# Attention scores and masks as 128x32 column tiles, score tiles apart within a turn, narrow diagonal blocks sharing a PSUM bank

## Chip, cores and metric

One Trainium2 chip, one of its NeuronCores. The metric is the device time of one execution in microseconds: the median of three runs of the kernel before is 1314.45 us (1314.13 to 1315.17).

## What is computed

`x` is (1, 2048, 128) in fp32. Six sublayers follow each other, each on a layer-normalised `x` and added to it; the two expert layers and the two ternary layers are weighted by 0.5:

```python
x = x + 0.5 * expert_ffn(layernorm(x), ...)      # 8 experts, top 1, gelu, then layernorm
x = x + attention0(layernorm(x), wq, wk, wv, wo, bo)
x = x + 0.5 * expert_ffn(layernorm(x), ...)
x = x + 0.5 * ternary_ffn(layernorm(x), ...)
x = x + attention1(layernorm(x), W, b)           # no output projection
x = x + 0.5 * ternary_ffn(layernorm(x), ...)
```

Both attentions have 16 heads of dimension 8 over 2048 positions and are causal:

```python
scores = einsum('bhqd,bhkd->bhqk', q, k)
scores = where(tril(ones((t, t), bool)), scores, -inf)
attn = softmax(scores / sqrt(8), axis=-1)
ctx = einsum('bhqk,bhkd->bhqd', attn, v)
```

## The kernel before, in words

The change lies in the two calls of `attention_layer`. Its heads are worked in four groups of four (`G`), its queries in four chunks of 512 (`CH`, `NCH`); a pair of group and chunk (g, c) is a *step*. `STEPS` has 16 of them: chunks 0 to 3 for groups 0 and 1, then chunks 3 to 0 for groups 2 and 3.

Queries and keys lie in `q_slots` and `k_slots` as fp16 parts, 32 partitions (`SLOT`) for each head of a group. In `k_slots` the rows of the three other heads are zero, so that a matmul over all 128 rows gives one head's scores.

A step needs two things.

*Maxima.* For each query of the step the largest score must be known before the exponentials. TensorE computes scores a first time with queries on the partitions, in *units* of one 128-query block, one head and up to 512 keys (`max_units_of`, line 1202; on the diagonal a mask matmul behind it, line 1205), and VectorE reduces each unit with a maximum (line 1317). A unit on the diagonal is 128, 256, 384 or 512 wide, with its block i. The maxima are turned by TensorE (line 1210), split into fp16 parts by VectorE and sent by DMA into spare rows of `q_slots`, from where the second score matmul subtracts them. Units go round a ring of three PSUM banks, 5 to 7 (`ring_item`): TensorE waits before a unit until the one three places earlier is read.

*Quads.* A quad is 128 keys for the 512 queries of the step, for its four heads; a step has 4(c+1) of them, the last four on the diagonal and 512, 384, 256 and 128 columns wide. `score_tile(q, pr)` computes scores of two heads with keys on the partitions, as two row tiles of 32 rows (line 1162), into two banks; diagonal ones get a mask matmul over all rows each (line 1169). ScalarE takes the exponential of both banks in one instruction (line 1279). `values(q)` multiplies with the values, four heads as column tiles of 9 columns, fp32, into one bank (line 1182). Score tiles alternate between two pairs of banks; a tile waits for the exponential of the tile two before (`exp_done`).

At the end of a step its output is copied by ScalarE (line 1287), turned by TensorE (line 1225), and scaled by VectorE (lines 1344 and 1348).

TensorE's order is written out in `TURNS`: one quad a turn, with some units of later steps. `units_beside_quads` deals them out: a unit costs `UNIT_FIXED` plus its columns, a quad `QUAD_FIXED` plus its columns, and the units of a step have to be done three quads (`SLACK`) before it begins. Units of the first two steps go ahead of all quads. In a turn stand the two score tiles, three quarters of the ring's items, the values of the quad before, and the last quarter. VectorE and ScalarE follow the same lists. Projections of queries, keys and values run ahead of the turns and beside the first of them.

Of the kernel before, what the change touches and what calls it, by code (L numbers as in the profile page):

```python
# [9 lines left out]
ALU = mybir.AluOpType  # L10
ACT = mybir.ActivationFunctionType
AX = mybir.AxisListType

P = 128
# [3 lines left out]
CH = 512  # L18
NCH = T // CH
BPC = CH // P  # L20
H = 16
DH = D // H
G = 4
# [10 lines left out]
TERMS = 3  # L34
Q_PARTS, K_PARTS = (0, 1, 0), (0, 0, 1)
SLOT = 32
MAX_ROW = TERMS * DH
MAX_PARTS = 2
MAX_UNIT = 16384.0
# [23 lines left out]
def macaron_layers(nc, x_in, wq, wk, wv, wo, bo, wr, w1, b1, wo2, bo2, gamma, beta,  # L63
# [16 lines left out]
    with stack:  # L80
        blk = stack.enter_context(nc.Block())
        psum = stack.enter_context(nc.psum_tensor("psum", [P, 8, CH], F32))
# [924 lines left out]
                [(g, c) for c in reversed(range(NCH)) for g in range(HALF, NG)]  # L1007
        AHEAD = 2
        SLACK = 3
        UNIT_FIXED, QUAD_FIXED = 64, 64  # L1010

        def quads_of(step):
            return [(step, j) for j in range(BPC * (step[1] + 1))]

        def max_units_of(step):

            return [(step, i, kc, h) for i in range(BPC) for kc in range(step[1] + 1) for h in range(G)]

        def columns_of_quad(q):
            (_, c), j = q  # L1020
            return CH - max(0, j - BPC * c) * P

        def columns_of_unit(u):
            (_, c), i, kc, _ = u
            return CH if kc < c else (i + 1) * P

        def units_beside_quads():

# [31 lines left out]
        def attention_layer(proj, layer, projected, given, next_norms, next_given, released):  # L1060
# [17 lines left out]
            def rows_of(h):  # L1078
                return slice(SLOT * h, SLOT * (h + 1))

# [58 lines left out]
            for (_, units), (_, turn_max, _, turn_out) in zip(TURNS, PLAN):  # L1139
# [3 lines left out]
                for item in RING_ITEMS[-1]:  # L1143
                    ring_no[item] = len(ring_no)
            last_unit = {s: max(n for item, n in ring_no.items() if item[0] == "scores" and item[1][0] == s)
                         for s in STEPS}

            @blk.tensor
            def _(pe):
                def score_tile(q, pr):  # L1150

                    (g, c), j = q
                    n = quad_no[q]
                    off = first_query(q)
                    if j == 0 and pr == 0:
                        pe.wait_ge(negmax_landed[step_no[q[0]] % 4], 16 * MAX_PARTS * (step_no[q[0]] // 4 + 1))
                    tile = 2 * n + pr
                    if tile >= 2:
                        pe.wait_ge(exp_done, tile - 1)
                    for par in range(2):  # L1160
                        rows = rows_of(2 * pr + par)
                        last = pe.matmul(psum[:, S_BANKS + 2 * (tile % 2) + par, off:CH],  # L1162
                                         k_slots[rows, G * g + 2 * pr + par, j * P:(j + 1) * P],
                                         q_slots[rows, g, c * CH + off:(c + 1) * CH],
                                         start=True, stop=q not in diagonal)
                    if q in diagonal:

                        for par in range(2):
                            last = pe.matmul(psum[:, S_BANKS + 2 * (tile % 2) + par, off:off + P],  # L1169
                                             ident_bf[:, :], later_keys[:, :], start=False, stop=True)  # L1170
                    last.then_inc(scores_done, 1)

                def values(q):

                    (g, c), j = q
                    n = quad_no[q]
                    off = first_query(q)
                    pe.wait_ge(exp_done, 2 * n + 2)
                    if j == 0:
                        pe.wait_ge(*((out_copied, step_no[q[0]]) if step_no[q[0]] else (o_bank_set, 1)))  # L1180
                    for h in range(G):
                        last = pe.matmul(psum[VW * h:VW * h + DH + 1, O_BANK, off:CH],  # L1182
                                         v_aug[:, j, G * g + h, :],
                                         probs[:, (2 * n + h // 2) % NP, h % 2, off:CH],
                                         start=(j == 0), stop=(j == BPC * (c + 1) - 1))
                    last.then_inc(pv_done, 1)

                def ring_item(item):
                    kind, what = item
                    n = ring_no[item]  # L1190
                    bank = RING_BANKS + n % RING
                    if n >= RING:
                        pe.wait_ge(ring_read, n - RING + 1)
                    if kind == "scores":
                        (g, c), i, kc, h = what
                        if (g, i, kc, h) == (0, 0, 0, 0):
                            pe.wait_ge(q_landed[c], 16 if c else 16 * (G + 1))
                            if c:
                                pe.wait_ge(k_landed[c - 1], 16 * G)
                        w = CH if kc < c else (i + 1) * P  # L1200
                        qb = BPC * c + i
                        last = pe.matmul(psum[:, bank, 0:w], q_slots[:, g, qb * P:(qb + 1) * P],  # L1202
                                         k_slots[:, G * g + h, kc * CH:kc * CH + w], start=True, stop=kc < c)
                        if kc == c:
                            last = pe.matmul(psum[:, bank, i * P:w], later_keys[:, :], ident_bf[:, :],  # L1205
                                             start=False, stop=True)
                    elif kind == "max":
                        k = step_no[what]
                        pe.wait_ge(negmax_ready, k + 1)
                        last = pe.transpose(psum[0:G * BPC, bank, 0:P], neg_max[:, k % 2, :], ident[:, :])  # L1210
                    elif kind == "turned":
                        pe.wait_ge(ring_read, ring_no["out", (NG - 1, what)] + 1)
# [24 lines left out]
                for turn, ((q, _), items) in enumerate(zip(TURNS, RING_ITEMS)):  # L1237
                    if turn == LAST_PROJECTION:
                        proj.transposes(pe, NCH - 1)
                        proj.queries_keys(pe, NCH - 1)  # L1240
                        proj.values(pe, NCH - 1)
                    if turn == LAST_PROJECTION + 1:

                        pe.wait_ge(proj.lo_ready, 2 * NCH)
                        pe.wait_ge(proj.v_ready, NCH)

                    cuts = [0, 0, len(items) // 2 + len(items) // 4, len(items)]
                    if q:
                        score_tile(q, 0)
                    for item in items[cuts[0]:cuts[1]]:  # L1250
                        ring_item(item)
                    if q:
                        score_tile(q, 1)
                    for item in items[cuts[1]:cuts[2]]:
                        ring_item(item)
                    if previous:
                        values(previous)
                    for item in items[cuts[2]:cuts[3]]:
                        ring_item(item)
                    previous = q  # L1260

# [28 lines left out]
            def _(dve):  # L1290
# [8 lines left out]
                for turn, (items, (m_now, _, _, _)) in enumerate(zip(RING_ITEMS, PLAN)):  # L1299
# [8 lines left out]
                    for item in items:  # L1308
# [2 lines left out]
                        bank = RING_BANKS + n % RING  # L1311
                        dve.wait_ge(ring_full, n + 1)
                        if kind == "scores":
                            s, i, kc, h = what
                            dst = part_max[:, step_no[s] % 2, h, i, kc:kc + 1]
                            w = CH if kc < s[1] else (i + 1) * P
                            dve.tensor_reduce(dst, psum[:, bank, 0:w], axis=AX.X, op=ALU.max).then_inc(ring_read, 1)  # L1317
                        elif kind == "turned":
                            dve.tensor_copy(ctx_t[:, what * CH:(what + 1) * CH], psum[:, bank, :]).then_inc(ring_read, 1)
                        elif kind == "project":  # L1320
# [128 lines left out]
```

## Time and profile before

| | us |
|---|---|
| median of three runs | 1314.45 |
| profiled execution | 1314.37 |
| its span | 1312.6 |
| TensorE busy in it | 1186.3 |
| VectorE busy | 1033.5 |
| ScalarE busy | 668.8 |

The profile is of one execution. Busy is the time covered by an engine's instructions; matmuls are pipelined and their ends modelled, so that the distance between two starts says more than the length of one. TensorE's granted clock was 0.97 of the full one in the mean. The first attention layer covers about 191 to 652 us of the span, the second 835 to 1290 us.

### The profile page before, as it was taken

The numbers are of one execution on the slowest core, as the hardware profiler recorded it, in microseconds if no ns is written. First come the engines' busy times: TensorE is split into PE (matmuls) and PEld (weight loads), VectorE is DVE, ScalarE is ACT, GpSimd is POOL, SyncE is SP. The second block draws the span as 40 slices with busy tenths as digits, with TensorE's granted clock in tenths as the row PEclk, the third lists the DMA queues.
The fourth block names the chain that finished last, engine by engine and source line by source line (L and its number), as shares of the span: only waits on it lengthen the run. The fifth ranks groups of instructions, "written<-read, shape, count | busy, mean of one in ns | idle before, by whom it ended". The sixth has DMA issues, their size and how long they took to land.

```text
span 1312.6 us, 21461 instructions
## 1 busy us (share of the span) xinstructions
PE 1186.3 (90%) x8293; PEld 461.7 (35%) x8293; DVE 1033.5 (79%) x2503; ACT 668.8 (51%) x861; POOL 65.3 (5%) x62
## 2 busy tenths in 40 slices
PE   1899968999999999999699979599999999999997
PEld 1455533222222222333355547232222222222336
DVE  8976487899999897875547566789999999877664
ACT  1322114555677667766332224145556667777663
POOL 5111010000000000000101000100000000000000
PEclk9999988999999999999799979799999999999999
DMA  4100141000000000000000000420000000000001
GB/s 147 33 1 1 48 121 57 1 2 1 2 1 1 2 1 1 1 1 2 1 0 1 1 0 25 146 57 1 1 2 1 1 1 1 1 1 2 1 2 33
DMA packets 23506, 23.26 MB, mean 18 GB/s; under 512 B 3134, under 2 KB 21220, under 8 KB 23404
## 3 DMA queue, kind: packets, MB, share of 16 engines
q1 hardware_dynamic: 22252, 18.73, 4.9%
q0 software_dynamic: 1152, 3.15, 0.9%
q8 instruction: 66, 1.08, 0.3%
q14 instruction: 36, 0.29, 0.1%
HBM read 13.20 MB, written 8.39 MB: 16 GB/s over the span
## 4 chain that ended last, share of the span: by engine, by line
PE 69%; DVE 25%; issue 2%; ACT 2%; DMA 1%; SPq 0%; DVEq 0%; ACTq 0%
PE psum L1182 19%; PE psum L1202 17%; DVE part_max L1317 14%; PE psum L442 9%; PE psum L1162 8%; PE psum L1169 4%; PE psum L466 2%; PE psum L898 2%; PE psum L1205 2%; PE psum L913 1%; DVE xn L167 1%; DVE norm_v L150 1%; PE psum L427 1%; DVE parts L838 1%; PE psum L1225 1%
## 5 line engine op out<-in xcount | busy, mean ns | idle before, releaser
L1317 DVE TENSOR_REDUCE part_max<-psum 128x1 f32<-128x512 f32 (+3 forms) x1280 | 703.5, 604 | 118.2 <-PE psum L1205 59.4
L1279 ACT ACTIVATE hidden<-psum 128x1024 f32<-128x1024 f32 (+3 forms) x640 | 542.4, 895 | 311.1 <-PE psum L1169 166.1
L1202 PE MATMUL psum<-k_slots,q_slots 128*128 128x512 f16 (+3 forms) x1280 | 396.8, 359 | 43.5 <-DVE part_max L1317 24.4
L1182 PE MATMUL psum<-hidden,v_aug 128*9 128x512 f32 (+3 forms) x2560 | 296.1, 535 | 0.0
L1202 PEld LDWEIGHTS psum<-k_slots,q_slots 128*128 128x128 f16 x1280 | 111.5, 97 | 402.0 <-DVE part_max L1317 320.0
L442 PE MATMUL psum<-parts,w_parts 128*128 128x512 f16 x768 | 177.6, 382 | 1.9 <-DVE parts L838 1.9
L1162 PE MATMUL psum<-q_slots,k_slots 32*128 32x512 f16 (+3 forms) x1280 | 163.9, 355 | 7.2 <-ACT hidden L1279 4.6
L1205 PE MATMUL psum<-ident_bf,later_keys 128*128 128x128 bf16 x512 | 111.0, 227 | 0.0
L442 PEld LDWEIGHTS psum<-parts,w_parts 128*128 128x128 f16 x768 | 73.2, 99 | 80.9 <-issue 3.0
L586 ACT CAST parts<-psum 128x512 f16<-128x512 f32 x64 | 37.2, 588 | 106.7 <-PE psum L427 106.7
L1162 PEld LDWEIGHTS psum<-q_slots,k_slots 32*128 32x128 f16 x1280 | 46.3, 91 | 109.4 <-issue 52.1
L1169 PE MATMUL psum<-later_keys,ident_bf 128*128 128x128 bf16 x512 | 73.8, 226 | 0.0
L1182 PEld LDWEIGHTS psum<-hidden,v_aug 128*9 128x9 f32 x2560 | 38.1, 88 | 72.3 <-issue 49.3
L838 DVE TENSOR_TENSOR parts<-parts 128x1024 f16<-128x1024 f16 x64 | 45.7, 738 | 18.3 <-ACT parts L586 18.2
L1205 PEld LDWEIGHTS psum<-ident_bf,later_keys 128*128 128x128 bf16 x512 | 51.9, 101 | 3.3 <-issue 0.3
L1169 PEld LDWEIGHTS psum<-later_keys,ident_bf 128*128 128x128 bf16 x512 | 29.2, 97 | 38.8 <-issue 27.1
L624 POOL TENSOR_TENSOR x_plus<-xn,bo_bc 128x512 f32<-128x512 f32 x8 | 13.8, 1720 | 566.1 <-DVE xn L167 527.4
L466 PE MATMUL psum<-wo_sb,hidden 128*128 128x128 f32 x256 | 33.3, 294 | 3.7 <-ACT hidden L577 3.7
L466 PEld LDWEIGHTS psum<-wo_sb,hidden 128*128 128x128 f32 x256 | 32.9, 209 | 5.6 <-ACT hidden L577 4.7
L953 POOL TENSOR_TENSOR x_plus<-x_res,fb_half 128x512 f32<-128x512 f32 x8 | 10.0, 1265 | 495.6 <-DVE xn L167 495.6
L244 ACT COPY xn_t<-psum 128x512 f32<-128x512 f32 x8 | 4.7, 587 | 58.2 <-PE psum L219 58.2
L675 DVE TENSOR_TENSOR x_plus<-psum,x_plus 128x512 f32<-128x512 f32 x8 | 5.5, 690 | 35.4 <-PE psum L466 35.4
(168 smaller groups left out, 735.7 us busy)
## 6 DMA issues: line engine op xcount, KB each, us to landing
q_slots<-q_rows SPq DMA_DIRECT2D x8, 512.0 KB, 3.8
k_slots<-k_rows POOLq DMA_DIRECT2D x24, 128.0 KB, 4.1
q_rows<-parts SPq DMA_DIRECT2D x18, 128.0 KB, 2.7
k_rows<-parts SPq DMA_DIRECT2D x18, 128.0 KB, 2.4
q_slots<-in_L_ffn_W_dram SPq DMA_DIRECT2D x2, 1024.0 KB, 6.6
k_slots<-k_rows SPq DMA_DIRECT2D x8, 128.0 KB, 4.0
q_slots<-nm_parts SPq DMA_DIRECT2D x64, 4.0 KB
out_dram<-x_res SPq DMA_DIRECT2D x4, 256.0 KB, 2.3
```

Source lines behind the costliest of these rows:

```text
L442: last = pe.matmul(psum[:, t, :], w1_parts[:, e, wp, t * P:(t + 1) * P], x_mask[:, k % NX, xp, :], start=(e == 0 and (wp, xp) == (0, 0)), ...
L466: last = pe.matmul(psum[:, DOWN_BANK, i * D:(i + 1) * D], hidden[:, n % 2, t, i * P:(i + 1) * P], wo2_sb[:, t, :], start=(t == 0), stop=(t ...
L586: act.copy(mask_sb[:, k % NX, :], psum[:, MASK_BANKS + k % 2, :]).then_inc(mask_ready, 1)
L838: dve.tensor_tensor(x_mask[:, k % NX, :, :], x_parts[:, n % 2, :, :], mask_sb[:, k % NX, :].rearrange("p (a t) -> p a t", a=1).broadcast_t ...
L898: last = pe.matmul(psum[:, 6 + n % 2, i * D:(i + 1) * D], hidden[:, n % 2, t, i * P:(i + 1) * P], tw2_t[:, t, :], start=(t == 0), stop=(t ...
L1162: last = pe.matmul(psum[:, S_BANKS + 2 * (tile % 2) + par, off:CH], k_slots[rows, G * g + 2 * pr + par, j * P:(j + 1) * P], q_slots[rows, ...
L1169: last = pe.matmul(psum[:, S_BANKS + 2 * (tile % 2) + par, off:off + P], ident_bf[:, :], later_keys[:, :], start=False, stop=True)
L1182: last = pe.matmul(psum[VW * h:VW * h + DH + 1, O_BANK, off:CH], v_aug[:, j, G * g + h, :], probs[:, (2 * n + h // 2) % NP, h % 2, off:CH] ...
L1202: last = pe.matmul(psum[:, bank, 0:w], q_slots[:, g, qb * P:(qb + 1) * P], k_slots[:, G * g + h, kc * CH:kc * CH + w], start=True, stop=kc ...
L1205: last = pe.matmul(psum[:, bank, i * P:w], later_keys[:, :], ident_bf[:, :], start=False, stop=True)
L1279: act.activation(probs[:, tile % NP, :, off:CH], psum[:, bank:bank + 2, off:CH], ACT.Exp, scale=scale).then_inc(exp_done, 1)
L1317: dve.tensor_reduce(dst, psum[:, bank, 0:w], axis=AX.X, op=ALU.max).then_inc(ring_read, 1)
```

## The change

- Every score matmul of attention, in units and in quads, and every mask matmul on it is split into four, one for each 32 columns of its stationary operand (`COLS` = 4), which go to the four quarters of the partitions. Quads use all 128 rows instead of 32.
- A score tile has the mask of its first head ahead of the scores of its second.
- On the diagonal, four heads of a 128-wide unit or two of a 256-wide one share a bank, with one mask matmul (of four tiles) and one reduce.
- In a turn: first score tile, a third of the ring's items, second score tile, a third, the values of the quad before, the last third.
- `UNIT_FIXED`, `QUAD_FIXED` go from 64, 64 to 100, 500, and a unit's columns include its mask and heads.

```diff
-        UNIT_FIXED, QUAD_FIXED = 64, 64
+        UNIT_FIXED, QUAD_FIXED = 100, 500
...
+        def unit_width(step, i, kc):
+
+            return CH if kc < step[1] else (i + 1) * P
+
         def max_units_of(step):
 
-            return [(step, i, kc, h) for i in range(BPC) for kc in range(step[1] + 1) for h in range(G)]
+            units = []
+            for i in range(BPC):
+                for kc in range(step[1] + 1):
+                    heads = CH // unit_width(step, i, kc)
+                    units += [(step, i, kc, h, heads) for h in range(0, G, heads)]
+            return units
...
         def columns_of_unit(u):
-            (_, c), i, kc, _ = u
-            return CH if kc < c else (i + 1) * P
+            step, i, kc, _, heads = u
+            return heads * (unit_width(step, i, kc) + (P if kc == step[1] else 0))
...
+            def rows32(m):
+                return slice(SLOT * m, SLOT * (m + 1))
+
+            def diagonal_part(rows, heads):
+
+                return rows.rearrange("p (a k) -> p a k", a=heads)[:, :, -P:]
+
+            def repeated(mask, heads):
+
+                return mask[:, :].rearrange("p (a k) -> p a k", a=1).broadcast_to([P, heads, P])
...
                     for par in range(2):
-                        rows = rows_of(2 * pr + par)
-                        last = pe.matmul(psum[:, S_BANKS + 2 * (tile % 2) + par, off:CH],
-                                         k_slots[rows, G * g + 2 * pr + par, j * P:(j + 1) * P],
-                                         q_slots[rows, g, c * CH + off:(c + 1) * CH],
-                                         start=True, stop=q not in diagonal)
-                    if q in diagonal:
-
-                        for par in range(2):
-                            last = pe.matmul(psum[:, S_BANKS + 2 * (tile % 2) + par, off:off + P],
-                                             ident_bf[:, :], later_keys[:, :], start=False, stop=True)
+                        bank = S_BANKS + 2 * (tile % 2) + par
+                        for m in range(COLS):
+                            last = pe.matmul(psum[rows32(m), bank, off:CH],
+                                             k_slots[:, G * g + 2 * pr + par, j * P + m * SLOT:j * P + (m + 1) * SLOT],
+                                             q_slots[:, g, c * CH + off:(c + 1) * CH],
+                                             start=True, stop=q not in diagonal)
+                        if q in diagonal:
+                            for m in range(COLS):
+                                last = pe.matmul(psum[rows32(m), bank, off:off + P],
+                                                 ident_bf[:, rows32(m)], later_keys[:, :], start=False, stop=True)
...
-                        last = pe.matmul(psum[:, bank, 0:w], q_slots[:, g, qb * P:(qb + 1) * P],
-                                         k_slots[:, G * g + h, kc * CH:kc * CH + w], start=True, stop=kc < c)
+                        for a in range(heads):
+                            for m in range(COLS):
+                                last = pe.matmul(psum[rows32(m), bank, a * w:(a + 1) * w],
+                                                 q_slots[:, g, qb * P + m * SLOT:qb * P + (m + 1) * SLOT],
+                                                 k_slots[:, G * g + h0 + a, kc * CH:kc * CH + w],
+                                                 start=(a == 0), stop=(kc < c))
                         if kc == c:
-                            last = pe.matmul(psum[:, bank, i * P:w], later_keys[:, :], ident_bf[:, :],
-                                             start=False, stop=True)
+                            for m in range(COLS):
+                                last = pe.matmul(diagonal_part(psum[rows32(m), bank, 0:heads * w], heads),
+                                                 later_keys[:, rows32(m)], repeated(ident_bf, heads),
+                                                 start=False, stop=True)
...
-                    cuts = [0, 0, len(items) // 2 + len(items) // 4, len(items)]
+                    cuts = [len(items) // 3, 2 * len(items) // 3]
...
-                            dst = part_max[:, step_no[s] % 2, h, i, kc:kc + 1]
-                            w = CH if kc < s[1] else (i + 1) * P
-                            dve.tensor_reduce(dst, psum[:, bank, 0:w], axis=AX.X, op=ALU.max).then_inc(ring_read, 1)
+                            w = unit_width(s, i, kc)
+                            dve.tensor_reduce(part_max[:, step_no[s] % 2, h0:h0 + heads, i, kc],
+                                              psum[:, bank, 0:heads * w].rearrange("p (a k) -> p a k", a=heads),
+                                              axis=AX.X, op=ALU.max).then_inc(ring_read, 1)
```

## Rows read from the trace of the kernel before

**Rows 1.** The page: busy time of each engine, share of span, instructions.
```profile
PE 1186.3 (90%) x8293; PEld 461.7 (35%) x8293; DVE 1033.5 (79%) x2503; ACT 668.8 (51%) x861; POOL 65.3 (5%) x62
```

**Rows 2.** The page: chain that ended last, by engine and by line.
```profile
PE 69%; DVE 25%; issue 2%; ACT 2%; DMA 1%; SPq 0%; DVEq 0%; ACTq 0%
PE psum L1182 19%; PE psum L1202 17%; DVE part_max L1317 14%; PE psum L442 9%; PE psum L1162 8%; PE psum L1169 4%; PE psum L466 2%; PE psum L898 2%; PE psum L1205 2%; PE psum L913 1%; DVE xn L167 1%; DVE norm_v L150 1%; PE psum L427 1%; DVE parts L838 1%; PE psum L1225 1%
```

**Rows 3.** Stretches of the second attention layer: length, busy us (instructions), clock, DMA share, GB/s.
```profile
835.00:862.00 27.00, 18.68 (x115) 7.76 (x115) 22.73 (x64) 7.78 (x10) 4.35 (x8) 0.87 0.39 107
862.00:889.10 27.10, 25.14 (x203) 8.61 (x195) 24.61 (x51) 12.93 (x18) 0.00 (x0) 1.00 0.02 4
889.10:940.30 51.20, 47.18 (x343) 14.47 (x340) 45.99 (x91) 28.00 (x36) 0.00 (x0) 1.00 0.01 1
940.30:1011.00 70.70, 67.84 (x486) 19.11 (x485) 65.69 (x123) 43.79 (x53) 0.00 (x0) 1.00 0.00 1
1011.00:1175.70 164.70, 161.86 (x1175) 43.87 (x1173) 146.93 (x268) 116.57 (x134) 0.00 (x0) 1.00 0.01 1
1175.70:1234.00 58.30, 57.22 (x449) 17.50 (x445) 45.02 (x90) 42.36 (x51) 0.00 (x0) 1.00 0.01 1
1234.00:1273.30 39.30, 37.27 (x333) 12.53 (x333) 22.88 (x72) 26.77 (x38) 0.59 (x1) 0.99 0.01 2
1273.30:1289.70 16.40, 11.89 (x74) 4.99 (x71) 12.04 (x60) 7.25 (x13) 3.21 (x3) 0.81 0.01 1
```

**Rows 4.** Groups by shape: count, busy us, mean ns of one, idle before, releasers.
```profile
L1317 DVE TENSOR_REDUCE part_max<-psum 128x1 f32<-128x512 f32 x896 | 566.9, 684 | 75.4 <-PE psum L1202 52.4 <-PE psum L1205 18.8
...
L1169 PE MATMUL psum<-later_keys,ident_bf 128*128 128x128 bf16 x512 | 73.8, 226 | 0.0
...
L1317 DVE TENSOR_REDUCE part_max<-psum 128x1 f32<-128x128 f32 x128 | 31.7, 285 | 15.6 <-PE psum L1205 15.1
```

**Rows 5.** Timeline of a c=3 turn: start us, us, engine, line, count, idle before.
```profile
1150.08 1.94 ACT L1279 ACTIVATE hidden<-psum 128x1024 f32<-128x1024 f32 x2 [0.75 <-PE psum L1162]
...
1150.30 0.12 PEld L1182 LDWEIGHTS psum<-hidden,v_aug 128*9 128x9 f32 x8 [0.23 <-issue]
...
1151.70 2.48 DVE L1317 TENSOR_REDUCE part_max<-psum 128x1 f32<-128x512 f32 x4 [0.36 <-PE psum L1202]
...
1151.82 0.65 PE L1162 MATMUL psum<-q_slots,k_slots 32*128 32x512 f16 x4
...
1152.24 1.02 ACT L1279 ACTIVATE hidden<-psum 128x1024 f32<-128x1024 f32 x1 [0.22 <-PE psum L1162]
```

**Rows 6.** Timeline of TensorE's matmuls alone through a full turn.
```profile
1044.98 1.04 PE L1182 MATMUL psum<-hidden,v_aug 128*9 128x512 f32 x8
1045.96 0.39 PE L1202 MATMUL psum<-k_slots,q_slots 128*128 128x512 f16 x1
1046.18 0.60 PE L1225 MATMUL psum<-ident,xn_t 128*128 128x128 f32 x4
1046.71 0.39 PE L1162 MATMUL psum<-q_slots,k_slots 32*128 32x512 f16 x4
1047.04 0.97 PE L1202 MATMUL psum<-k_slots,q_slots 128*128 128x512 f16 x3
1047.94 0.62 PE L1182 MATMUL psum<-hidden,v_aug 128*9 128x512 f32 x4
```

**Rows 7.** Chain of waits, in order of time: start us, us, what.
```profile
756.46 10.36 PE psum L442 x48
```

**Rows 8.** Timeline of TensorE's matmuls in a diagonal turn.
```profile
1261.53 0.39 PE L1162 MATMUL psum<-q_slots,k_slots 32*128 32x512 f16 x2
1261.85 0.29 PE L1169 MATMUL psum<-later_keys,ident_bf 128*128 128x128 bf16 x2
...
1262.60 0.41 PE L1182 MATMUL psum<-hidden,v_aug 128*9 128x128 f32 x8
```

**Rows 9.** Who waited for whom, 835 to 1290 us: total us, times, longest.
```profile
PEld psum L1202 <- DVE part_max L1317: 158.9, 303, 0.9
```

**Rows 10.** Stretch of the first attention layer, last two steps, columns as rows 3.
```profile
630.70:651.90 21.20, 15.95 (x106) 7.76 (x104) 9.98 (x34) 7.34 (x12) 3.69 (x3) 0.67 0.00 1
```

More of the change, by code:

```diff
@@ L36 @@
 SLOT = 32
+COLS = P // SLOT
 MAX_ROW = TERMS * DH
@@ L1194, in ring_item @@
                     if kind == "scores":
-                        (g, c), i, kc, h = what
-                        if (g, i, kc, h) == (0, 0, 0, 0):
+                        (g, c), i, kc, h0, heads = what
+                        if (g, i, kc, h0) == (0, 0, 0, 0):
                             pe.wait_ge(q_landed[c], 16 if c else 16 * (G + 1))
@@ L1199, in ring_item @@
                                 pe.wait_ge(k_landed[c - 1], 16 * G)
-                        w = CH if kc < c else (i + 1) * P
+                        w = unit_width(*what[:3])
                         qb = BPC * c + i
-                        last = pe.matmul(psum[:, bank, 0:w], q_slots[:, g, qb * P:(qb + 1) * P],
-                                         k_slots[:, G * g + h, kc * CH:kc * CH + w], start=True, stop=kc < c)
+                        for a in range(heads):
[4 more added lines that the diff above has]
+                                                 start=(a == 0), stop=(kc < c))
                         if kc == c:
-                            last = pe.matmul(psum[:, bank, i * P:w], later_keys[:, :], ident_bf[:, :],
-                                             start=False, stop=True)
+                            for m in range(COLS):
+                                last = pe.matmul(diagonal_part(psum[rows32(m), bank, 0:heads * w], heads),
+                                                 later_keys[:, rows32(m)], repeated(ident_bf, heads),
+                                                 start=False, stop=True)
                     elif kind == "max":
@@ L1245, in _ @@
                         pe.wait_ge(proj.v_ready, NCH)
-                    cuts = [0, 0, len(items) // 2 + len(items) // 4, len(items)]
+                    cuts = [len(items) // 3, 2 * len(items) // 3]
                     if q:
                         score_tile(q, 0)
-                    for item in items[cuts[0]:cuts[1]]:
+                    for item in items[:cuts[0]]:
                         ring_item(item)
@@ L1253, in _ @@
                         score_tile(q, 1)
-                    for item in items[cuts[1]:cuts[2]]:
+                    for item in items[cuts[0]:cuts[1]]:
                         ring_item(item)
@@ L1257, in _ @@
                         values(previous)
-                    for item in items[cuts[2]:cuts[3]]:
+                    for item in items[cuts[1]:]:
                         ring_item(item)
@@ L1313, in _ @@
                         if kind == "scores":
-                            s, i, kc, h = what
-                            dst = part_max[:, step_no[s] % 2, h, i, kc:kc + 1]
-                            w = CH if kc < s[1] else (i + 1) * P
-                            dve.tensor_reduce(dst, psum[:, bank, 0:w], axis=AX.X, op=ALU.max).then_inc(ring_read, 1)
+                            s, i, kc, h0, heads = what
+                            w = unit_width(s, i, kc)
+                            dve.tensor_reduce(part_max[:, step_no[s] % 2, h0:h0 + heads, i, kc],
+                                              psum[:, bank, 0:heads * w].rearrange("p (a k) -> p a k", a=heads),
+                                              axis=AX.X, op=ALU.max).then_inc(ring_read, 1)
                         elif kind == "turned":
```

## The prediction

> **What bounds the kernel now.** I read the busy shares first: TensorE is busy 90% of the span, VectorE 79%, ScalarE 51% [rows 1]. The chain of waits puts 69% on TensorE and 25% on VectorE; the ring's unit matmuls (L1202), the value matmuls (L1182), the score matmuls (L1162) and VectorE's reduce (L1317) lead it, all of them in attention [rows 2]. Then I cut the second attention layer into its stages [rows 3]: the run-in (835 to 862), the steps with c=0, c=1, c=2 of the first two groups, the four steps with c=3, and c=2, c=1, c=0 of the last two groups. From 862 to 1011 us VectorE is busy 90 to 93% of each stage and TensorE 92 to 96%; in the c=3 steps TensorE has 98%, VectorE 89%; behind them TensorE has 95 to 98% and VectorE 58 to 77%. So VectorE sets the pace early, TensorE late. Of VectorE's time the reduces are most: 684 ns for 512 columns, 285 for 128 [rows 4]; four in a row take 2.48 us, so one follows the other after (2.48-0.68)/3 = 0.60 us, some 0.08 before the other's end. I count 608 and 208 ns, and on the line between them 475 and 341 for 384 and 256 columns [rows 4, 5]. ScalarE needs 2 x 0.92 us of a full turn (two exponentials 1.94 us, one 1.02) [rows 5]; it bounds nothing but a short tail.
>
> The timeline of TensorE shows what a turn holds [rows 6]. 48 expert matmuls of 512 columns take 10.36 us, 0.213 us each: 2.4 columns a ns, the upper clock [rows 7]. Value matmuls are column tiles already: two groups of four take 1.04 us, one (cut by the window's end) 0.62, so a group follows another after some 0.43 us. 512 fp32 columns stream 0.427 (two passes: transposes of 128 fp32 columns follow each other after 0.109): four tiles cost what one does, and a few ns, 7 by the 1.04 us of the eight. The four score matmuls are row tiles, and also run together: from their start to the next unit 0.33 us, of which 0.213 is stream. The rest is the price of changing the tiling: about 0.10 us each time. Transposes to scores (0.53 - 0.44), scores to unit (0.33 - 0.21), and values to unit (0.98 - 0.87) agree [rows 6].
>
> **The change, part by part.** The counts are worked out from the code's planner and its two cost formulas; per layer there are 16 steps, 160 turns, of them 64 diagonal.
>
> (1) Tiling changes. A turn with units has four (rows, full, columns, full), a diagonal one two more, because a mask lies between score tiles [rows 8]. That makes 752 a layer before, 74 us at 98 ns, some 147 us in both. After, only transposes and projections are of another tiling: I keep 0.65 us a step for them (0.44 stream, two changes).
>
> (2) Score matmuls. Four heads at once become four heads one after the other, each as a group of four column tiles over all 128 rows. A full turn streams 4 x 0.213 instead of 0.213: +0.64 us, less four changes (0.39): +0.25. Diagonal turns paired only two heads and so go from 2w to 4w columns: for w = 512 from 1.07 us ([rows 8], 1261.53 to 1262.60) to (2048+512)/2.4 = 1.07, so the wide one gains just the two changes around the values, and narrower ones more. Over a layer score streams go from 51 to 130 us (masks in both).
>
> (3) Unit matmuls. Columns stay: four tiles together stream what one 128-wide matmul did. Units per layer go from 640 to 560, since four 128-wide or two 256-wide heads share a bank. A reduce over four blocks costs 608 ns instead of 4 x 208, over two blocks 608 instead of 2 x 341: 0.30 us less a step, 5 us a layer, of VectorE. If the blocks cost the reduce something, the bound is the four short ones, so between 0 and 5.
>
> (4) Group overhead. A layer will have about 2030 groups of four. Between value groups 7 ns are over the stream, between full matmuls 2 [rows 6, 7]; I take 5, so 10 us a layer. Bounds: 2 ns (4 us), and 28 ns, if each of four tiles added its 7 (57 us). The values' eight loads come within 0.12 us, of which 0.09 is one [rows 5]: 4 ns for 9 columns, so 32 columns may need 16 and a group 64, where 128-column groups (some 510 a layer) stream 53; at worst 6 us of the 10.
> The Trainium skill (TensorEngine Tiling (Array Packing), Restrictions) says that column tiling turns fast weight load off, and TensorE: Matmul & The Clock Gate (LDWEIGHTS) gives P/1.2 ns for P columns. By that 32 columns take 27 ns; what it would do is rival C.
>
> (5) The order. Score tiles stand a third of the turn's units apart, and the values behind two thirds. Today the second tile sometimes waits for the exponential of the turn before: four score matmuls then cover 0.65 us instead of 0.39 [rows 5, 6]. After, the tiles are over 0.6 us apart and ScalarE needs 0.92, within a turn of 2.4: this goes. The planner's new costs (100 and 500) give a diagonal quad more weight, so units come evenly: 3 to 5 a turn in the c=3 steps, where now one turn has 7 and another 2. TensorE's loads for units stand 159 us of the layer behind the reduce [rows 9]; most is cover by matmuls in flight, but bursts of units against a 0.6 us reduce are what makes TensorE stop.
>
> **The sum**, second layer. TensorE's load is stream (columns by 2400 a us), changes and 0.65 a step, after with 5 ns a group. The c=3 steps show it: before 51.5 units + 17.9 scores + 49.5 values + 288 changes, 28.2, + 2.6 = 149.8 (rounded); after 52.1 + 52.9 + 49.5 + 2.6 + 747 groups, 3.7 = 160.8. In a c=2 stage scores and changes go from 7.3 + 11.0 to 19.6, in late c=1 from 5.5 + 7.8 to 12.8; values (17.9 and 11.1) stay, units move by under 1. Run-in and first c=0, 54.1 us: reduces 35.1 before, 35.5 after; no change. First c=1, 51.2: reduces 42.9 to 43.9, TensorE 42 to 43: no change, the even order against 1 us more. First c=2, 70.7: reduces 61.5 to 59.1, TensorE 60.3 to 62.7, so both near 63: -1.5. The c=3 steps, 164.7: TensorE 149.8 to 160.8, VectorE busy 146.9 as before. This stage is now 15 us above its heavier load, 0.23 us a turn, in waits of the kind of (5); I let it be 5 above after (0.08 a turn, a choice: the waits of single score tiles and bursts go): 166, +1.3. Late c=2, 58.3: TensorE 53.1 to 55.4, 5.2 above becomes 1.8: -1.1. Late c=1, 39.3: 34.5 to 34.1, 4.8 above becomes 2.2: -3. Last c=0, 16.4: 11.2 to 10.6 and no split waits: -1. That is -5.3 a layer; the first layer has a longer tail (21 us for 16 [rows 10]), so -6.5 there. Sum -12. Nothing outside attention changes. The profiled execution took 1314.37 us around its span of 1312.6 and lies within 0.1 us of the median, so 1314.4 - 12 = **1302**.
>
> **Rivals.**
> A, the forecast: 1302, own range 1288 to 1312.
> B, more is won: groups cost 2 ns and TensorE runs nearly without waits. 6 us a layer from the groups, 5 from the c=3 steps: 1302 - 24 = 1278. For: late stages at 98% busy. Against: early VectorE sets the time.
> C, weights late (slower). Where a 128-column group streams 53 ns and the next group's four loads take longer, TensorE waits. At twice the 53, 510 groups x 54 ns = 27 us a layer, of which some 60% where TensorE decides: 1302 + 33 = 1335. For: the second of two masks starts 0.29 - 0.226 = 0.064 us behind the first, where it streams 0.053: a load that was not ready shows [rows 4, 8]. Against: the 4 ns of nine columns [rows 5]. It makes the change a loss from 10 ns over the stream a group, about. This is also where the skill's 27 ns a load lead; no run here shows it yet.
> D, waits stay (slower). TensorE's added 11 us in the c=3 steps come on top of unchanged waits: +11 there, +2.3 late c=2, +1 first c=2, 0 elsewhere: +13 a layer, 1340. It decides from 0.16 us of waits a turn. For: each TensorE stop on the ring also delays scores that stand behind it. Against: the waits come with bursts.
> E, instruction rate. A layer will hold 8,130 matmuls and as many loads, 16,260 instructions for 6,140: one in 26 ns over its 427 us, against 70 now; a narrow diagonal turn about 110 in 1.5 us. Nothing in the trace shows sequences that dense for long; eight loads in 0.12 us show it only for a short one. At 32 ns each a layer takes 520 us and the kernel about 1500; if only diagonal turns are held (28 ns x 110 = 3.1 us, +0.7 for each of 128) 1302 + 90 = 1392, which I take. That fp16 column tiles did not run together at all would cost far more (every score and unit stream fourfold); the fp32 ones speak against it.
> The skill (TensorE: Matmul & The Clock Gate, Part 2) names some 62 ns a MATMUL where the sequencer's microcode decodes; 8,130 of them would be 504 us a layer. Nothing here tells whether that path is on.
> F, nothing moves: loads trade evenly, 1314.
>
> **Chances.** A 0.47 (0.42 faster, 0.05 same), B 0.15, C 0.10, D 0.15 (0.02 of it same), E 0.08, F 0.05. Under 0.2%, 2.6 us, a measurement can't tell the kernels apart: faster 0.57, same 0.12, slower 0.31. The range 1274 to 1342 leaves E and a strong B out.
>
> **What would show it.** TensorE from a unit to scores or values with no 0.1 us over the stream; groups 218 ns apart at 512 columns and 58 at 128 (C: over 80); a full turn with three units near 2.4 us; single score tiles never waiting for ScalarE; reduces of 512 columns at 600 ns with four outputs; late c=1 near 36 us, c=3 near 166. The prediction is wrong if c=3 steps lengthen by over 5 us a layer (D, or C if narrow groups are late), or if gaps appear between groups that wait for nothing (E).

## The result and the profile after

The changed kernel takes 1263.18 us (median of 4 runs, 1262.68 to 1264.19) against 1314.29: a ratio of 0.9619, 95% interval [0.9595, 0.9644], 51 us less. 1302 was forecast, and 1274 was the low end of the range: the direction was right, the size four times too small.

The page of the profile after (span 1260.9 us): busy time by engine; chain that ended last.

```profile
PE 1160.4 (92%) x18405; PEld 589.2 (47%) x18405; DVE 1017.0 (81%) x2343; ACT 670.0 (53%) x861; POOL 65.4 (5%) x62
...
PE 70%; DVE 24%; issue 2%; ACT 2%; DMA 1%; SPq 0%; DVEq 0%; ACTq 0%
```

TensorE holds 18,405 matmuls instead of 8,293 and is busy for less time [rows 1]; the two engines share the chain as before [rows 2].

The stages of the second attention layer (columns as in rows 3). Here and in rows 3 every cut lies 11.1 us behind the first exponential of the stage's first step, in the kernel before and in the changed one alike. So the lengths are those from one first exponential to the next, but the busy times belong to a stretch that lies 11.1 us late:

```profile
832.90:857.00 24.10, 23.16 (x493) 10.90 (x485) 23.59 (x46) 13.56 (x18) 0.00 (x0) 1.00 0.03 7
857.00:904.50 47.50, 46.30 (x938) 21.29 (x938) 46.07 (x84) 28.23 (x35) 0.00 (x0) 1.00 0.01 3
904.50:969.70 65.20, 64.75 (x1238) 28.90 (x1230) 61.59 (x109) 42.75 (x52) 0.00 (x0) 1.00 0.01 3
969.70:1131.50 161.80, 161.52 (x3016) 73.01 (x3012) 147.42 (x251) 117.02 (x134) 0.00 (x0) 1.00 0.01 3
1131.50:1187.40 55.90, 55.74 (x1155) 26.77 (x1151) 43.38 (x76) 41.53 (x50) 0.00 (x0) 1.00 0.01 3
1187.40:1222.10 34.70, 33.59 (x814) 17.47 (x806) 20.97 (x59) 27.32 (x39) 0.66 (x1) 1.00 0.02 4
1222.10:1236.00 13.90, 9.47 (x113) 4.61 (x112) 11.49 (x56) 6.38 (x11) 3.14 (x3) 0.72 0.00 1
```

Against [rows 3] each stage is shorter:

| stage | forecast | measured |
|---|---|---|
| first c=0 | 0 | 27.1 to 24.1: -3.0 |
| first c=1 | 0 | 51.2 to 47.5: -3.7 |
| first c=2 | -1.5 | 70.7 to 65.2: -5.5 |
| c=3, four steps | +1.3 | 164.7 to 161.8: -2.9 |
| late c=2 | -1.1 | 58.3 to 55.9: -2.4 |
| late c=1 | -3 | 39.3 to 34.7: -4.6 |
| last c=0 | -1 | 16.4 to 13.9: -2.5 |

That is -24.6 for this layer where I had -5.3; the first layer went from 437 to 412 us, and some 2 us more lie outside the two.

Cut at the exponentials themselves, the first three stages together ("early" below) and the c=3 steps are, before:

```profile
850.87:999.84 148.97, 138.58 (x1004) 42.02 (x1003) 134.59 (x259) 80.75 (x101) 2.17 (x4) 1.00 0.05 14
999.84:1164.53 164.69, 161.93 (x1175) 44.19 (x1175) 148.30 (x273) 115.86 (x133) 0.00 (x0) 1.00 0.01 1
```

and after:

```profile
821.78:958.54 136.76, 133.60 (x2737) 61.47 (x2732) 131.78 (x237) 81.84 (x101) 2.17 (x4) 1.00 0.06 17
958.54:1120.31 161.77, 161.48 (x3015) 73.17 (x3010) 147.93 (x252) 115.74 (x132) 0.00 (x0) 1.00 0.01 3
```

Early, VectorE's busy time fell from 134.6 to 131.8 us, and its idle time from 14.4 to 5.0.

TensorE's matmuls in a full turn of the c=3 steps of the changed kernel (start us, us, engine, line, count):

```profile
1021.75 1.03 PE L1203 MATMUL psum<-hidden,v_aug 128*9 128x512 f32 x8
1022.61 0.60 PE L1225 MATMUL psum<-k_slots,q_slots 128*32 128x512 f16 x8
1023.04 0.60 PE L1184 MATMUL psum<-q_slots,k_slots 128*32 128x512 f16 x8
1023.47 0.39 PE L1225 MATMUL psum<-k_slots,q_slots 128*32 128x512 f16 x4
1023.69 0.60 PE L1184 MATMUL psum<-q_slots,k_slots 128*32 128x512 f16 x8
```

From the values to the unit are 0.86 us, which is the stream of two fp32 groups (2 x 0.427) and nearly nothing else; two fp16 groups take 0.43, one 0.21 to 0.22. No change of tiling is left ([rows 6]: 0.98, 0.33). And the narrowest diagonal turn of a late c=1 step, where 128-column groups follow each other:

```profile
1208.93 0.23 PE L1231 MATMUL psum<-ident_bf,later_keys 128*32 128x128 bf16 x4
1208.99 0.23 PE L1184 MATMUL psum<-q_slots,k_slots 128*32 128x128 f16 x4
1209.04 0.23 PE L1190 MATMUL psum<-later_keys,ident_bf 128*32 128x128 bf16 x4
...
1209.38 0.23 PE L1190 MATMUL psum<-later_keys,ident_bf 128*32 128x128 bf16 x4
1209.43 0.60 PE L1203 MATMUL psum<-hidden,v_aug 128*9 128x256 f32 x8
```

Nine groups, 36 matmuls and 36 loads, take 0.50 us: 55 ns a group of 53 ns of stream, 7 ns an instruction. With this, rival C (loads late, over 80 ns a group) and rival E (26 ns an instruction too dense) are out. The reduce takes the shared banks at the price of a full one (count, busy us, mean ns, idle before):

```profile
L1343 DVE TENSOR_REDUCE part_max<-psum 128x1 f32<-128x512 f32 x896 | 564.9, 683 | 52.5 <-PE psum L1225 28.5 <-PE psum L1231 16.6
...
L1343 DVE TENSOR_REDUCE part_max<-psum 128x2 f32<-128x512 f32 x64 | 42.6, 686 | 9.3 <-PE psum L1231 8.7
...
L1343 DVE TENSOR_REDUCE part_max<-psum 128x4 f32<-128x512 f32 x32 | 22.1, 689 | 9.5 <-PE psum L1231 9.3
```

Two or four outputs instead of one cost 3 and 6 ns.

### The profile page after: what moved, and what is told of

It is laid out like the page before. It is cut to its first block, busy times and chain, and to the rows that moved or that the text cites. A ratio compares the mean times of both kernels' runs of the same rounds, so it can differ in the third digit from the quotient of the medians.

```text
span 1260.9 us, 41528 instructions
## 1 busy us (share of the span) xinstructions
PE 1160.4 (92%) x18405; PEld 589.2 (47%) x18405; DVE 1017.0 (81%) x2343; ACT 670.0 (53%) x861; POOL 65.4 (5%) x62
## 4 chain that ended last, share of the span: by engine, by line
PE 70%; DVE 24%; issue 2%; ACT 2%; DMA 1%; SPq 0%; DVEq 0%; ACTq 0%
PE psum L1203 16%; PE psum L1184 15%; DVE part_max L1343 14%; PE psum L1225 13%; PE psum L443 11%; PE psum L467 3%; PE psum L899 2%; PE psum L1231 2%; PE psum L1190 1%; PE psum L914 1%; PE psum L1252 1%; DVE xn L168 1%; PE psum L428 1%; DVE norm_v L151 1%; ACT hidden L1306 1%
## 5 line engine op out<-in xcount | busy, mean ns | idle before, releaser
L1343 DVE TENSOR_REDUCE part_max<-psum 128x1 f32<-128x512 f32 (+3 forms) x1120 | 688.9, 668 | 86.0 <-PE psum L1231 48.0
L1225 PE MATMUL psum<-k_slots,q_slots 128*32 128x512 f16 (+3 forms) x5120 | 410.4, 353 | 20.5 <-DVE nm_parts L1364 7.1
L1184 PE MATMUL psum<-q_slots,k_slots 128*32 128x512 f16 (+3 forms) x5120 | 355.8, 349 | 4.5 <-ACT hidden L1306 1.4
L1225 PEld LDWEIGHTS psum<-k_slots,q_slots 128*32 128x32 f16 x5120 | 130.8, 97 | 244.7 <-DVE part_max L1343 126.5
L1184 PEld LDWEIGHTS psum<-q_slots,k_slots 128*32 128x32 f16 x5120 | 127.8, 97 | 105.1 <-ACT hidden L1306 15.9
L1190 PE MATMUL psum<-later_keys,ident_bf 128*32 128x128 bf16 x2048 | 103.2, 220 | 0.0
L1231 PE MATMUL psum<-ident_bf,later_keys 128*32 128x128 bf16 (+2 forms) x1408 | 92.1, 252 | 0.0
L1203 PEld LDWEIGHTS psum<-hidden,v_aug 128*9 128x9 f32 x2560 | 61.3, 91 | 41.1 <-issue 1.5
L1190 PEld LDWEIGHTS psum<-later_keys,ident_bf 128*32 128x32 bf16 x2048 | 55.1, 97 | 13.8
L1231 PEld LDWEIGHTS psum<-ident_bf,later_keys 128*32 128x32 bf16 x1408 | 38.6, 100 | 28.9 <-issue 18.1
```

The source lines that it names most:

```text
L1184: last = pe.matmul(psum[rows32(m), bank, off:CH], k_slots[:, G * g + 2 * pr + par, j * P + m * SLOT:j * P + (m + 1) * SLOT], q_slots[:, g, ...
L1190: last = pe.matmul(psum[rows32(m), bank, off:off + P], ident_bf[:, rows32(m)], later_keys[:, :], start=False, stop=True)
L1225: last = pe.matmul(psum[rows32(m), bank, a * w:(a + 1) * w], q_slots[:, g, qb * P + m * SLOT:qb * P + (m + 1) * SLOT], k_slots[:, G * g + ...
L1231: last = pe.matmul(diagonal_part(psum[rows32(m), bank, 0:heads * w], heads), later_keys[:, rows32(m)], repeated(ident_bf, heads), start=Fa ...
L1343: dve.tensor_reduce(part_max[:, step_no[s] % 2, h0:h0 + heads, i, kc], psum[:, bank, 0:heads * w].rearrange("p (a k) -> p a k", a=heads), ...
```

## The experiments

All ratios are to the kernel before, run on the same chip; the brackets are 95% intervals, so that a difference of two ratios is uncertain by 4 to 5 us. "Early" is the stretch from the second layer's first exponential to the first of its c=3 steps: 149.0 us in the kernel before, of them 14.4 in which VectorE idles, and 136.8 and 5.0 in the changed one.

### The changed kernel less one part

**The turn's order put back.**

```diff
-                    cuts = [len(items) // 3, 2 * len(items) // 3]
+                    cuts = [0, 0, len(items) // 2 + len(items) // 4, len(items)]
```

(and the old loop over them)

> The changed kernel (1263) with only the turn's order put back: both score tiles first, three quarters of the items, values, the last quarter. Theory 1 (the new order evens what reaches VectorE, and that took its idle time out of the early stages): VectorE's idle in the stages c=0, c=1, c=2 of the first groups, 5 us a layer in the changed kernel against 13 before, comes back, and single score tiles wait for ScalarE again: 1263 + 2 x 8 + 4 = about 1283. Rival 2 (the lost tiling changes alone shortened the blocks between units, so the order is worth nothing): within 4 us of 1263.

Measured 1274.9 us, ratio 0.9726 [0.9701, 0.9752]: some 14 us lost, between the two. Early 139.4 us, VectorE idle 7.7; the c=3 steps 163.0. The order is worth something, but seven tenths of the early idle time that went stay away without it. The weight loads of the score tiles wait 24 us for ScalarE instead of 16 over the whole run.

**The planner's old costs.**

```diff
-        UNIT_FIXED, QUAD_FIXED = 100, 500
+        UNIT_FIXED, QUAD_FIXED = 64, 64
...
-            return heads * (unit_width(step, i, kc) + (P if kc == step[1] else 0))
+            return heads * unit_width(step, i, kc)
```

> The changed kernel with the planner's old costs (64 and 64, a unit's mask not counted). Theory 1 (even numbers of units a turn matter): turns with 6 to 8 units beside turns with 2 return and with them waits on the ring, some 3 us a layer early and 2 late: about 1273. Rival 2 (the ring and VectorE's pace smooth it anyway): within 4 us of 1263.

1260.3 us, 0.9609 [0.9587, 0.9631]: no loss. Theory 1 is wrong here; the even numbers of units that I counted on buy nothing.

**One head to a bank.**

```diff
-                    heads = CH // unit_width(step, i, kc)
+                    heads = 1
```

> The changed kernel with one head to a bank for every unit, as before. VectorE gets back 5 us of reduces a layer, of which about half falls where VectorE sets the time: theory 1 expects 1263 + 2 x 3 = 1269. Rival 2 (shared banks also hold more work in the ring of three, and that took VectorE's idle out of the early stages): 1263 + 2 x (3 + 6) = about 1281.

1274.0 us, 0.9717 [0.9693, 0.9741]: 13 us lost, between the two. Early 140.8 us, but idle 5.0: in the new tiling the banks' part shows as VectorE's busy time (135.8 against 131.8), not as idle.

**Full matmuls, no column tiles.**

```diff
-                        for m in range(COLS):
-                            last = pe.matmul(psum[rows32(m), bank, off:CH],
-                                             k_slots[:, G * g + 2 * pr + par, j * P + m * SLOT:j * P + (m + 1) * SLOT],
+                        last = pe.matmul(psum[:, bank, off:CH],
+                                         k_slots[:, G * g + 2 * pr + par, j * P:(j + 1) * P],
```

(and so for masks and units)

> The changed kernel with units and scores as full 128x128 matmuls over 128 rows; the values stay column tiles. Same stream, a quarter of the matmuls, two changes of tiling a turn (into and out of the values). If a change of tiling costs 0.1 us and nothing else differs: TensorE's load +160 x 0.196 = 31 us a layer, of which the late 22 us count in full and the early third: 1263 + 2 x 25 = 1313, that is about the time of before. Rival (four column tiles give more than the absence of changes, or less): below 1295 if the changes hide under waits.

1307.7 us, 0.9952 [0.9933, 0.997]: 44 us lost, 50 expected. Early and the c=3 steps:

```profile
847.32:989.29 141.97, 139.31 (x984) 53.97 (x983) 133.22 (x237) 81.75 (x101) 2.17 (x4) 1.00 0.05 14
989.29:1162.28 172.99, 172.99 (x1152) 60.82 (x1151) 148.78 (x252) 115.75 (x132) 0.00 (x0) 1.00 0.01 1
```

Early, VectorE idles 8.8 us. TensorE is busy without a gap in the c=3 steps, +11.2 us for 64 turns with two changes, 0.175 us a turn. Column tiles are not faster than one full matmul (the same stream); they pay because the values are column tiles in any case and everything else can then be too.

**Only the units full.** As above, for units and their masks alone.

> The changed kernel with only the units as full matmuls, the scores left as column tiles: up to six changes of tiling a turn. TensorE's load +160 x 0.59 = 94 us a layer, less in the last turns without units: 1263 + 2 x 75 = about 1410. If the changes cost TensorE only where it would not wait anyway: 1340 to 1380.

1418.4 us, 1.0797 [1.0776, 1.0819], two executions: near the 1410 expected for up to six changes a turn.

### The kernel before with one part

**The order alone** (the first edit of this section the other way round, on the old tiling).

> The kernel before with only the new order of a turn, its tiling kept. Row tiles of the four heads no longer run together: each full turn streams scores twice (+0.213 us) and changes tiling twice more (+0.20). TensorE's load rises by 96 x 0.41 + 64 x 0.2 (diagonal turns: two changes back and forth with units between tiles), 40 to 52 us a layer, partly under VectorE early: 1314 + 2 x 35 = about 1385. Rival: the even order wins back what VectorE waits early (13 us a layer): 1314 + 2 x 22 = 1358.

1345.8 us, 1.0245 [1.0224, 1.0265], two executions: slower, and less so than either said. The same edit costs 32 us on row tiles and gives 14 on column tiles. On row tiles, setting the score tiles apart gives up that four heads run together: in its trace two heads' score matmuls take 0.33 us up to the next unit, as all four do in [rows 6], and the c=3 steps go from 164.7 to 176.6 us.

**The costs alone.**

> The kernel before with only the planner's new costs (100 and 500, mask columns counted). In the changed kernel the old costs were worth nothing (1260 against 1263), so theory 1: 1308 to 1315, no gain. Rival (with the old tiling, where blocks between units are longer, even turns matter): 1300 or less.

1310.5 us, 0.9977 [0.9961, 0.9992]: about nothing, as theory 1 said.

**Costs and shared banks** on the old tiling and order.

> The kernel before with the planner's new costs and shared banks, and with its own tiling (row tiles for scores, full matmuls for units and masks) and its own order in a turn: all of the change but the tiling and the order. If the tiling and the order make the gain: 1305 to 1312, only VectorE's 5 us of reduces a layer and some evenness. If planner and banks made most of it: 1280 or less.

1289.5 us, 0.9829 [0.9796, 0.9862], between the two. It is nearly half of the whole gain, without one more column tile. The parts' prices depend on what else is there and don't add: taken out of the changed kernel one at a time, tiling (44), order (14) and banks (13) come to 71 us, and the whole is 51.

**Shared banks alone** (with one mask and one reduce a bank).

```diff
-            return [(step, i, kc, h) for i in range(BPC) for kc in range(step[1] + 1) for h in range(G)]
+                    heads = CH // unit_width(step, i, kc)
+                    units += [(step, i, kc, h, heads) for h in range(0, G, heads)]
```

> The kernel before with only the shared banks for narrow diagonal units, its own costs, tiling and order. Theory 1: packing made nearly all of the 24 us of planner and banks together (1289), half of it reduces (5 us a layer of VectorE), half because three banks of narrow units hold 0.6 us of VectorE's work where a values block with its changes takes 1.05 us, and three full ones hold 1.8: 1288 to 1294, idle of VectorE in the early stages 9 us a layer instead of 14. Rival (the reduces alone count): 1303 or more, idle unchanged.

1288.1 us, 0.9816 [0.9788, 0.9844]: 25 us by this part alone (the traced execution, 1282.1 us, is the fastest of four). Early and the c=3 steps:

```profile
831.18:974.04 142.86, 135.64 (x979) 41.19 (x978) 132.57 (x234) 80.92 (x101) 2.18 (x4) 1.00 0.05 14
974.04:1135.52 161.48, 160.28 (x1151) 43.41 (x1151) 146.09 (x249) 115.76 (x133) 0.00 (x0) 1.00 0.01 1
```

Early it takes 142.9 us instead of 149.0: 2 us less of VectorE's busy time (132.6) and 4 less of its idle time (10.3). The c=3 steps went from 164.7 to 161.5.

**Shared banks, each head reduced by itself.** Is it VectorE's load or the ring?

```diff
-                            dve.tensor_reduce(part_max[:, step_no[s] % 2, h0:h0 + heads, i, kc],
-                                              psum[:, bank, 0:heads * w].rearrange("p (a k) -> p a k", a=heads),
-                                              axis=AX.X, op=ALU.max).then_inc(ring_read, 1)
+                            for a in range(heads):
+                                last = dve.tensor_reduce(part_max[:, step_no[s] % 2, h0 + a, i, kc:kc + 1],
+                                                         psum[:, bank, a * w:(a + 1) * w], axis=AX.X, op=ALU.max)
+                            last.then_inc(ring_read, 1)
```

> The kernel before with shared banks (1288), but VectorE reduces every head of a shared bank by itself, four short reduces instead of one, so that its load is that of the kernel before and only the ring differs. Theory 1 (a bank holds more work, and TensorE waits less often): 1288 + 2 x 3 = 1294. Rival 2 (the load of the reduces makes the gain): 1303 or more.

> The changed kernel (1263) in the same way: shared banks, every head reduced by itself. With single heads to a bank it was 1274. Theory 2 (in the new tiling VectorE sets the time early and its load is what counts): 1271 to 1276. Theory 1 (the ring): 1263 to 1268.

On the old tiling 1293.7 us, 0.9823 [0.9796, 0.9851]: within the intervals the same as with one reduce (0.9816). In the traces the two attention layers together take 864.7 us before, 843.7 here and 838.5 with one reduce. So the reduces' load is worth some 1 to 5 us there, and 20 or more come with single reduces too. VectorE's idle time shows where. In the kernel before, 128-wide units had 15.6 us in front of them [rows 4], and 256-wide ones:

```profile
L1317 DVE TENSOR_REDUCE part_max<-psum 128x1 f32<-128x256 f32 x128 | 47.5, 416 | 12.9 <-PE psum L1205 12.7
```

Here (old tiling, shared banks, single reduces):

```profile
L1341 DVE TENSOR_REDUCE part_max<-psum 128x1 f32<-128x512 f32 x896 | 567.0, 684 | 68.1 <-PE psum L1223 46.9 <-PE psum L1228 16.9
...
L1341 DVE TENSOR_REDUCE part_max<-psum 128x1 f32<-128x256 f32 x128 | 46.5, 416 | 6.5 <-PE psum L1228 5.7
L1341 DVE TENSOR_REDUCE part_max<-psum 128x1 f32<-128x128 f32 x128 | 28.1, 282 | 10.0 <-PE psum L1228 9.7
```

Over all widths and both layers the idle time in front of reduces fell from 118.1 to 99.2 us, 12 of the 19 before the narrow ones.

On the new tiling 1268.4 us, 0.9649 [0.9629, 0.967]: between 0.9717 (one head to a bank) and 0.9619 (one reduce for all), some 9 us for the shared banks with single reduces and 4 for the reduces, the latter within the intervals. That the 9 us are the ring's is not shown: early, VectorE idles 4.8 us here and 5.0 with one head to a bank, and what differs is its busy time (133.4 and 135.8).

### A kernel faster than both

The loads say that TensorE sets the c=3 steps of the changed kernel (159 us of load, 161.8 of time) and that a full turn's scores take 0.85 us there, where four row tiles would take 0.21 and two changes of tiling 0.20.

```diff
+                        if q not in diagonal:
+                            rows = rows_of(2 * pr + par)
+                            last = pe.matmul(psum[:, S_BANKS + 2 * (tile % 2) + par, :],
+                                             k_slots[rows, G * g + 2 * pr + par, j * P:(j + 1) * P],
+                                             q_slots[rows, g, c * CH:(c + 1) * CH],
+                                             start=True, stop=True)
+                            continue
```

(in those turns both score tiles stand first)

> The changed kernel, but in turns off the diagonal the scores are four row tiles at once again, both score tiles first; two changes of tiling a turn instead of 0.64 us of stream: -0.44 us in each of 96 turns a layer. Theory (TensorE sets the late stages, VectorE the early ones): c=3 steps from 162 to about 152 us, late c=2 from 56 to 51, late c=1 from 34.6 to 32, nothing early: 1263 - 2 x 17 = about 1229. Rival (two adjacent tiles wait for ScalarE and bursts return, as in the order of before): 1255 to 1270.

1229.4 us, 0.9345 [0.9322, 0.9368]: the total that was worked out from the loads. Early, the c=3 steps, late c=2 and late c=1:

```profile
806.48:939.98 133.50, 127.52 (x2441) 53.77 (x2433) 130.66 (x236) 81.53 (x101) 2.18 (x4) 1.00 0.06 17
939.98:1091.04 151.06, 148.94 (x2436) 57.32 (x2436) 145.11 (x253) 115.92 (x133) 0.00 (x0) 1.00 0.01 2
1091.04:1144.31 53.27, 51.61 (x930) 21.11 (x930) 44.04 (x77) 42.23 (x51) 0.00 (x0) 1.00 0.01 3
1144.31:1178.46 34.15, 32.33 (x708) 15.65 (x707) 22.22 (x42) 26.51 (x34) 0.00 (x0) 1.00 0.01 3
```

The c=3 steps take 151.1 us (152 expected). VectorE is busy for 145.1 of them, and TensorE's load is by estimate some 138 (159 less 48 turns x 0.44), so VectorE's is now the heavier one here too. The other stages did not come out as expected, and it is luck that the total did: late c=2 and c=1 gave 2.7 and 0.5 us where 5 and 2.6 were expected, and early, where nothing was, 3.3 went, with VectorE's idle time down to 2.8 us. That is the mistake of the prediction once more. Two trials on top of it:

> The kernel with row tiles for the scores of full quads (1229) with the planner's old costs. Full quads are cheaper there, so equal costs for narrow and full quads fit less badly: 1222 to 1230. If the planner matters more where VectorE sets the time in the c=3 steps too: up to 1235.

1226.7 us, 0.9346 [0.9313, 0.9379].

> The same kernel (1229) with units due two quads ahead of their step instead of three: the same work spread over 1 quad more. If the maxima then come late for the first quad of a step, each step waits about 1 us: 1245. If the DMA of the maxima still lands in time: 1226 to 1229.

1227.1 us, 0.9345 [0.9321, 0.9368]. Neither differs from it.

## Why the prediction was wrong

Two terms failed, the rule for the early stages in the sum and the price of the shared banks in step 3; in both VectorE's idle time was left out.

**Step 1, tiling changes: right.** 0.1 us each, and all but those around transposes gone; full matmuls beside column-tile values cost back 44 us.

**Step 2, score streams: right.** Two heads' scores take 0.43 us where they stream 0.427. The 34 us of row tiles in full turns confirm only the direction: -0.44 us in 96 turns would be 84 us in two layers. In the c=3 steps they won half of their 21 us, up to where VectorE's load is the heavier one.

**Step 3, shared banks: failed.** I priced them as reduces alone (5 us a layer), and in the early stages not even those, as the planner moved units about. On the old tiling they are worth 25 us, 20 or more of it with VectorE's reduces left single; in the changed kernel 13, 9 of it so. What I did not price shows, on the old tiling, as 19 us less idle time in front of reduces. My explanation is the ring: a narrow unit fills one of three banks with 0.2 us of VectorE's work, so three hold 0.6, while values and their two changes keep TensorE away for 1.05 us [rows 6]; a shared bank holds 0.6 by itself. Fewer items also change how the planner deals units out, and the runs don't separate that from what a bank holds; and in the new tiling the gain is not in idle time. So how much of it is the ring stays open.

**Step 4, group overhead: mis-sized.** 5 ns a group was taken, 2 to 3 is measured: 2 us in the c=3 steps, 5 a layer. The loads of a 32-column group were ready even under 53 ns of stream. By an estimate from the Trainium skill (TensorE: Matmul & The Clock Gate, LDWEIGHTS) four loads of 27 ns would have taken 107 ns a group, had they come one after another; the trace has 55, so they don't add up that way.

**Step 5, the order: right in kind, wrong in place.** The thirds are worth 14 us in the changed kernel. Of the second layer's 5.3 us, 2.6 are early, where I had written "no change" and where VectorE idles 2.7 us less for them; I had looked for them in the c=3 steps (1.2) and behind. The planner's costs, which I gave a share of it, are worth nothing (0.9609 and 0.9977).

**The sum: the rule for the early stages failed, the largest miss.** Early, 12.2 us were won where 1.5 was forecast, over half of the 19.3 us missed in this layer. For each stage I kept what it had above its heavier load, and let it shrink only late. "VectorE sets the pace early" was read as "VectorE's load is the time". It had 14.4 us of idle time in 149, of which the trace puts 13.4 to reduces that wait for TensorE, and a change that frees TensorE there pays as well: 9 us of idle went in this layer, of the 12 won early, and the waits fell to 3.8. Tiling and order each take some of it: with full matmuls 8.8 us of idle time are left, with the old order 7.7, in the changed kernel 5.0. In the c=3 steps the time above TensorE's load went from 15 us to 3, where I had 5.

**Slips in the working.** The stretches of rows 3 lie 11.1 us behind the steps that I named after them. L442, which stands ahead of L1162 in the chain of rows 2, is an expert matmul and not attention. In (3) a step has two pairs of 256-wide banks, not one: 0.37 us of reduces a step, 6 us a layer. Rival B's terms add up to 22 us, not 24 (1280), and rival D's to 14.3 a layer, not 13 (1343). None of them changes the verdict.

Rival B (more is won) came nearest, 1278, with its 0.15; its argument against itself, that VectorE sets the time early, was the same mistake. C and E are refuted by the timelines above, D by the c=3 steps, which got 2.9 us shorter.

## What to carry to other kernels

Where two engines are both 90% busy in a stage, neither load is its time: list the idle time of the one that leads and who ends it, and give a change a share of that too. Check that a stage is cut where its steps begin before you read busy and idle time from it. Count a ring by the work that its slots hold, not by slots; that slots with a quarter of the work run dry behind a block that full ones bridge is argued here, not shown by itself. If one kind of matmul must be tiled by columns, tiling the others alike costs nothing in stream and saves 0.1 us a change; where a kind could run four at a time on row tiles, two changes are cheaper than 0.64 us of stream.

## What the hardware did unexpectedly

TensorE took 72 instructions in 0.50 us, 7 ns each, and 16,000 a layer at one in 25 ns, while it was busy for 161.5 of the 161.8 us of the c=3 steps. Four 32-column loads for each group stayed hidden behind 53 ns of stream. Four column tiles of 512 fp16 columns take 0.21 to 0.22 us together, as one full matmul does.
